# Attention output kept by token tiles and turned 128 channels at a time, with bias products once a bank and the last output projection by halves

## What is computed

```
x = x + 0.5 * ffn0(layernorm(x))          # ternary weights, silu gate, rms norm
x = x + attention0(layernorm(x))          # causal, ALiBi bias
x = x + 0.5 * ffn0(layernorm(x))
x = x + 0.5 * ffn1(layernorm(x))          # 2:4 sparsity of the hidden activations
x = x + attention1(layernorm(x))          # causal, rotary positions, biases on q, k, v and the output
x = x + 0.5 * ffn1(layernorm(x))

attention: q, k, v = projections of x                      (16 heads of 16 channels)
           p = softmax(q k^T / 4 + bias + causal mask)
           y = p v                                         (2048 x 256, heads side by side)
           out = y Wo (+ bo in attention1)
```

## Time and profile before

| | |
|---|---|
| median of three runs | 1694.61 us |
| the profiled execution | 1705.08 us, of which the span from first to last instruction is 1703.2 us |
| PE busy | 1543.7 us, 91% of the span |
| DVE, ACT, POOL busy | 73%, 56%, 12% |
| mean granted clock of PE | 0.945 of full speed |
| last places, tail and chain of the first attention | 632.94 to 701.82 us |
| the same of the second attention | 1467.44 to 1546.58 us |

### The profile page before, as it was taken

The page is one execution under the profiler, slowest core; times in us unless marked ns, Lnnn a source line. Parts: engine busy times, 40 slices in busy tenths (PEclk is TensorE's granted clock), DMA queues, the critical chain, the costliest instruction groups (busy, mean ns, idle before and its releaser), DMA issues. The chain is left out here.

```text
span 1703.2 us, 32639 instructions
## 1 busy us (share of the span) xinstructions
PE 1543.7 (91%) x13324; PEld 973.4 (57%) x13324; DVE 1242.4 (73%) x1735; ACT 945.8 (56%) x1891; POOL 208.7 (12%) x275
## 2 busy tenths in 40 slices
PE   2798788989999999899899598899999999998997
PEld 0687654444434446688688586544444444556887
DVE  7766457888898873566588886677888988433897
ACT  5454334757768875565344222456687688653442
POOL 0243000000000000156001032000000002200000
PEclk9999959999999999999999897779999999988999
DMA  5001969000000000200100076831101000000000
GB/s 212 25 0 15 186 148 127 26 13 25 14 13 14 2 2 1 75 1 1 37 1 1 16 140 179 106 51 46 47 24 32 14 2 2 2 1 1 2 25 26
DMA packets 38197, 70.61 MB, mean 41 GB/s; under 512 B 5490, under 2 KB 13298, under 8 KB 37236
## 3 DMA queue, kind: packets, MB, share of 16 engines
q1 hardware_dynamic: 38052, 68.58, 18.1%
HBM read 48.90 MB, written 22.15 MB: 42 GB/s over the span
## 5 line engine op out<-in xcount | busy, mean ns | idle before, releaser
L1333 DVE TENSOR_REDUCE l_att_maxima<-psum 128x2 f32<-128x1024 f32 (+3 forms) x640 | 665.2, 1063 | 141.0 <-PE psum L1130 132.5
L1501 ACT ACTIVATE l_att_probs<-psum 128x512 f32<-128x512 f32 (+3 forms) x1280 | 604.0, 532 | 287.0 <-PE psum L1160 266.0
L1177 PE MATMUL psum<-l_att_probs,l_att_v 128*17 128x256 f32 (+2 forms) x4608 | 353.1, 383 | 0.6
L1160 PE MATMUL psum<-l_att_qt,l_kt 51*128 51x512 f32 (+6 forms) x1280 | 318.2, 459 | 6.9 <-ACT l_att_probs L1501 6.7
L1130 PE MATMUL psum<-l_kt,l_att_qt 59*128 59x512 f32 (+7 forms) x1280 | 287.9, 427 | 5.1 <-DVE l_att_maxima L1333 3.3
L1160 PEld LDWEIGHTS psum<-l_att_qt,l_kt 59*128 59x128 f32 (+1 forms) x1280 | 137.1, 192 | 152.7 <-ACT l_att_probs L1501 141.2
L1177 PEld LDWEIGHTS psum<-l_att_probs,l_att_v 128*17 128x17 f32 x4608 | 82.1, 96 | 145.0 <-issue 93.6
L1130 PEld LDWEIGHTS psum<-l_kt,l_att_qt 59*128 59x128 f32 (+1 forms) x1280 | 140.9, 202 | 19.2 <-DVE l_att_maxima L1333 17.7
L358 PE MATMUL psum<-xh,w_ternary 128*128 128x512 f32 x256 | 104.0, 406 | 21.0 <-PEq L165 16.3
L1127 PE MATMUL psum<-tri 64*128 64x128 bf16 x1024 | 90.3, 240 | 24.4 <-DVE l_att_maxima L1333 17.4
L1456 POOL CAST l_att_crow<-l_att_cneg 128x16 bf16<-128x16 f32 x32 | 8.1, 254 | 807.6 <-DVE l_att_cneg L1343 807.6
(11 more groups left out here) (204 smaller groups left out, 2527.9 us busy)
## 6 DMA issues: line engine op xcount, KB each, us to landing
l_kt<-qk_scratch SPq DMA_DIRECT2D x48, 256.0 KB, 10.6
qk_scratch<-l_att_kv_parts SPq DMA_DIRECT2D x22, 512.0 KB, 8.6
l_att_qt<-qk_scratch SPq DMA_DIRECT2D x168, 64.0 KB
qk_scratch<-y SPq DMA_DIRECT2D x10, 512.0 KB, 13.4
set_raw<-in_w_gu SPq DMA_DIRECT2D x2, 1024.0 KB, 6.8
y<-in_w_gu SPq DMA_DIRECT2D x1, 2048.0 KB, 8.5
y<-in_rope SPq DMA_DIRECT2D x8, 256.0 KB, 6.4
l_att_w_raw<-in_w_gu SPq DMA_DIRECT2D x4, 512.0 KB, 3.8
```

Source lines behind the costliest of these rows:

```text
L1160: e.matmul(g.ps[:, score_bank(i), off:BLK], g.kt[rows_of(x), hp, kt * P:(kt + 1) * P], qt[rows_of(x), hp, off:BLK], start=u >= TPB, stop=True,
L1177: ins = e.matmul(g.ps[h * VW:h * VW + HD + 1, OB, lo:hi], g.v[:, kt, STEPS[st][1] * HG + h, :], pr[:, un % PB, h, lo:hi], start=u == 0 and ...
L1333: e.tensor_reduce(mp[:, st % 2, 2 * p:2 * p + 2, t, c], g.ps[:, bank:bank + 2, 0:w], AX.X, ALU.max).then_inc(s.mx, 1)
L1501: e.activation(pr[:, un % PB, h, off:BLK], g.ps[:, score_bank(i), off:BLK], ACT.Exp, scale=HD ** -0.5).then_inc(s.ex, 1)
```

## The change

It has four parts.

- `y` is laid out as 16 token tiles of 256 channels. `normalise` writes four pieces of 64 channels, 256 apart, for a step, and `turn` transposes a full 128x128 piece: four transposes give what eight products with the identity gave. A turn needs both head groups, so the turns of block 0 stand at the last two places ahead of the tail, and those of the other blocks at u = 2, 7, 12 (first 128 channels) and u = 5, 10 (the others), the latter ahead of the unit's `values`.
- In the second attention a bias product fills a whole bank of two token tiles (512 columns, the bias row read twice), and is the first product of the bank instead of the last of each tile. That holds for v and for the output.
- The last 128 channels of the last block (both groups, 14 and 15) go through transposes, `last_normalise`, turn, ACT copy, `last_split` and products in two halves of two token tiles, in banks of their own.
- The layer norm's turn moves from u = 10 to between the last two `values`. On DVE its statistics come after `split_turned(1, 1)`, its scaling (L128) after `split_turned(2, 1)`.

```
                 dst = g.ps[:, 6 + j // 2, (j % 2) * D:(j % 2 + 1) * D]
+                if rope and j % 2 == 0:
+                    e.matmul(g.ps[:, 6 + j // 2, :].rearrange("p (a d) -> p a d", a=2), g.one_row[:, :],
+                             g.brow[:, 0:D].unsqueeze(1).broadcast_to([HALF // 2 + 1, 2, D]),
+                             start=True, stop=False, skip_group_check=True)
                 todo = [(k, w, x) for k in range(KD) for w, x in terms]
                 for q, (k, w, x) in enumerate(todo):
                     ins = e.matmul(dst, xp[x][b % 2][:, k, j * P:(j + 1) * P], wq[w][:, k, 2 * D:3 * D],
-                                   start=q == 0, stop=not rope and q == len(todo) - 1)
-                if rope:
-                    ins = e.matmul(dst, g.one_row[:, :], g.brow[:, 0:D], start=False, stop=True)
+                                   start=q == 0 and not rope, stop=q == len(todo) - 1, skip_group_check=rope)
...
-        SHARED = ("T00", "T01", "O00", "T10", "O01", "Y14", "T11", "O10", "T20", "O11", "T21", "N0", "N1",
-                  "O20", "T30", "O21", "T31", "Y15")
+        SHARED = ("T00", "T01", "O00", "T10", "O01", "Y14", "T11", "O10", "T20", "O11", "T21", "O20", "T30", "O21",
+                  "N0", "N1", "U0", "U1")
+        HALVES = (slice(0, BLK // 2), slice(BLK // 2, BLK))
+        Y15 = (SB - 1, 2 * SB)
...
+        def heads_out(st, tiles):
+
+            qb, hg = STEPS[st]
+            rows = slice(qb * TPB + tiles[0], qb * TPB + tiles[-1] + 1)
+            return g.y[:, rows, hg * HG * HD:(hg + 1) * HG * HD].rearrange("p t (h d) -> p t h d", h=HG)
...
-            def turn(b, group, tiles):
-
-                item = f"T{b}{group // KD}"
-                r = group % (NG // KD) * HG * HD
-                if group % (NG // KD) == 0 and tiles[0] == 0:
-                    open_shared(item)
+            def turn_tiles(b, k, tiles, bank):
+
                 for j in tiles:
-                    ins = e.matmul(g.ps[r:r + HG * HD, shared_bank(item), j * P:(j + 1) * P], yv[:, b, group, j, :],
-                                   g.ident[:, :], start=True, stop=True)
-                if group % (NG // KD) and tiles[-1] == TPB - 1:
-                    ins.then_inc(s.yt, 1)
-                    released[item] = (s.ylo, KD * b + group // KD + 1)
+                    ins = e.transpose(g.ps[:, bank, j * P:(j + 1) * P],
+                                      g.y[:, b * TPB + j, k * P:(k + 1) * P], g.ident[:, :])
+                ins.then_inc(s.yt, 1)
+
+            def turn(b, k):
+
+                item = f"T{b}{k}"
+                turn_tiles(b, k, range(TPB), open_shared(item))
+                released[item] = (s.ylo, KD * b + k + 1)
+
+            def out_bias(bank):
+
+                e.matmul(g.ps[:, bank, :].rearrange("p (a d) -> p a d", a=2), g.one_row[:, :],
+                         g.brow[:, D:2 * D].unsqueeze(1).broadcast_to([HALF // 2 + 1, 2, D]),
+                         start=True, stop=False, skip_group_check=True)
 
             def out_product(b, j, bank, parts):
 
+                if rope and j % 2 == 0 and 0 in parts:
+                    out_bias(bank)
...
-                                       start=k == 0 and q == 0 and j % 2 == 0,
-                                       stop=not rope and k == KD - 1 and q == 2, skip_group_check=True)
-                if rope and KD - 1 in parts:
-                    ins = e.matmul(g.ps[:, bank, (j % 2) * D:(j % 2 + 1) * D], g.one_row[:, :], g.brow[:, D:2 * D],
-                                   start=False, stop=True, skip_group_check=True)
+                                       start=not rope and k == 0 and q == 0 and j % 2 == 0,
+                                       stop=k == KD - 1 and q == 2, skip_group_check=True)
...
-                if p >= 2 * TAIL - NG:
-                    turn(0, p - 2 * TAIL + NG, range(TPB))
+                if p >= 2 * TAIL - KD:
+                    turn(0, p - 2 * TAIL + KD)
...
+                if q == 0 and 0 < b < NB - 1:
+                    turn(b, 1)
                 if u:
                     values(un - DELAY, 0)
                 values(un - DELAY, 1)
                 if q == 2:
-                    turn(b + 1, 0, range(TPB))
-                    turn(b + 1, 1, range(TPB))
-                if q == 4 and b < NB - 2:
-                    turn(b + 1, 2, range(TPB))
-                    turn(b + 1, 3, range(TPB))
+                    turn(b + 1, 0)
                 if u == 3:
                     output_transposes(NS - 2, open_shared("Y14"))
                     released["Y14"] = (s.mx, read)
-                if u == 10:
-                    normal_turn(0)
-                    normal_turn(1)
-                if u == 14:
-                    turn(NB - 1, 2, range(TPB))
-            for un in range(UNITS - DELAY, UNITS):
-                values(un, 0)
-                values(un, 1)
+            values(UNITS - DELAY, 0)
+            values(UNITS - DELAY, 1)
+            normal_turn(0)
+            normal_turn(1)
+            values(UNITS - 1, 0)
+            values(UNITS - 1, 1)
             e.wait_ge(s.ylo, KD * NB - 1)
             for j in range(TPB):
                 out_product(NB - 1, j, j // 2, range(1))
-            output_transposes(NS - 1, open_shared("Y15"))
-            e.wait_ge(s.mx, read)
-            turn(NB - 1, 3, range(TPB))
-            e.wait_ge(s.ylo, KD * NB)
-            for j in range(TPB):
-                out_product(NB - 1, j, j // 2, range(1, KD))
+            e.wait_ge(s.ose, NS)
+            for half in range(2):
+                for t in range(2 * half, 2 * half + 2):
+                    ins = e.transpose(g.ps[:, Y15[half], t * P:(t + 1) * P], osb[:, t * P:(t + 1) * P], g.ident[:, :])
+                ins.then_inc(s.oth, 1)
+            for half in range(2):
+                e.wait_ge(s.yl, half + 1)
+                turn_tiles(NB - 1, 1, range(2 * half, 2 * half + 2), open_shared(f"U{half}"))
+            for half in range(2):
+                e.wait_ge(s.ylo, KD * NB + half)
+                for j in range(2 * half, 2 * half + 2):
+                    out_product(NB - 1, j, half, range(1, KD))
...
+            def last_normalise(half):
+
+                tiles = slice(2 * half, 2 * half + 2)
+                e.wait_ge(s.oth, half + 1)
+                po = g.ps[:, Y15[half], HALVES[half]].rearrange("p (t h w) -> p t h w", t=TPB // 2, h=HG)
+                e.reciprocal(rinv[:, tiles, :], po[:, :, :, HD]).then_inc(s.ri, 1)
+                e.wait_ge(s.ri, NS + half)
+                yv = heads_out(NS - 1, range(2 * half, 2 * half + 2))
+                e.tensor_tensor(yv, po[:, :, :, 0:HD], rinv[:, tiles, :].unsqueeze(3).broadcast_to([P, TPB // 2, HG, HD]),
+                                ALU.mult).then_inc(s.yl, 1)
+
+            def last_split(half):
+
+                hi, lo = out_parts(NB - 1, KD - 1)
+                e.wait_ge(s.yhi, KD * NB + half)
+                e.tensor_tensor(lo[:, HALVES[half]], g.ps[:, shared_bank(f"U{half}"), HALVES[half]], hi[:, HALVES[half]].bitcast(F32),
+                                ALU.subtract).then_inc(s.ylo, 1)
...
+            split_turned(1, 1)
             e.wait_ge(s.xres, 2)
             dve_stats(e, g, ln, 1, 0)
-            split_turned(1, 1)
-            dve_normalise(e, g, ln, 1, 0)
             residual(1, 0, shared_bank("O10"))
             split_turned(2, 0)
             residual(1, 1, shared_bank("O11"))
             split_turned(2, 1)
-            split_normal(0)
-            split_normal(1)
+            dve_normalise(e, g, ln, 1, 0)
             residual(2, 0, shared_bank("O20"))
             split_turned(3, 0)
             residual(2, 1, shared_bank("O21"))
-            normalise(NS - 1, shared_bank("Y15"))
-            split_turned(3, 1)
+            split_normal(0)
+            split_normal(1)
+            for half in range(2):
+                last_normalise(half)
+            for half in range(2):
+                last_split(half)
...
-            e.wait_ge(s.yt, KD * NB)
             e.wait_ge(s.po, 2 * (NB - 1))
-            e.activation(out_parts(NB - 1, KD - 1)[0], g.ps[:, shared_bank("T31"), :], ACT.Copy).then_inc(s.yhi, 1)
+            for half in range(2):
+                e.wait_ge(s.yt, KD * NB + half)
+                e.activation(out_parts(NB - 1, KD - 1)[0][:, HALVES[half]], g.ps[:, shared_bank(f"U{half}"), HALVES[half]],
+                             ACT.Copy).then_inc(s.yhi, 1)
...
-        g.y = sb("y", [P, NB * NG * TPB, HG * HD], F32)
+        g.y = sb("y", [P, NT, D], F32)
```

More of the change, by code:

```diff
@@ L963, in attention_phase @@
 def attention_phase(nc, g, name, rope, a, qx, splits, small, loads=()):
-    names = "ql qnext qrest amm mx cfin cm cp ct ctc cdma st ex pv ose ot ri yt yhi ylo po xres"
+    names = "ql qnext qrest amm mx cfin cm cp ct ctc cdma st ex pv ose ot ri yt yhi ylo po xres oth yl"
     names += " wraw whi wlo" if loads else ""
@@ L1213, in open_shared @@
                 return shared_bank(item)
```

(33 more changed lines are left out.)

## The result

The changed kernel took 1678.55 us (median of 4 runs, 1677.55 to 1681.10) against 1696.48 (4 runs, 1693.83 to 1699.49) of the kernel before on the same chip: a ratio of 0.988, 95% interval 0.985 to 0.991. Run again beside the experiments it took 1674.35 us (6 runs, 1664.71 to 1683.41), ratio 0.986 (0.982 to 0.990). The forecast was 1665, the range 1654 to 1681: faster and inside the range, but 9 to 14 us above the number.

A forecast was written before the change was run, and what follows sets the result against it. PE was taken to bound the tails, and latency the last chain. Two attentions at 11.1 us plus 4.3 for biases give 26.5, with 3 for clock: 1694.6 - 26.5 - 3 = 1665 us, range 1654 to 1681.

The forecast's parts named there:

- last chain: End of each attention, from step 15's transposes to the last addition: in halves 4.5 us instead of 6.32, gain 1.8.
- rival B: Four transposes of `y` cost 1.02 us like eight products, and halves give nothing: 1681 us, chance 0.11.
- turns ahead of the tail: Last four places before each attention's tail: two without a turn, two with four transposes, 5.2 instead of 8.0 us.
- tail with u = 6: Each attention's tail: cheaper turns gain 5.7 us, and a shorter wait in the scores of u = 6 gains 0.8.
- one attention: Sum for the first attention, 2.8 + 5.7 + 0.8 + 1.8 = 11.1 us; the second the same before its biases.
- biases of v: Second attention's v projection: one bias product for two tiles saves 0.39 us a bank, 2.3 us in three blocks.
- biases in the tail: Second attention's tail: gain between 0 and 0.39 us a bank, middle 0.2 taken for six banks, 1.2 us.
- biases in the chain: Second attention's last chain: four biases (2.0 us) leave, two of 0.61 come ahead of the transposes, gain 0.8 us.
- I take 3 us of these 11 as gain: Half-clock stretches in both tails and around the second chain's end cost 11 us; 3 us of it counted as gained.
- Rival A: The clock stays up in the tails and at the second chain's end, gaining all 11 us: 1657 us, chance 0.17.
- Rivals C and D: C: transposes cost clock at some turns, 1690, chance 0.05. D: lower clock through both tails, 1786 or 1727, chance 0.03.

The follow-up runs named there:

- biases alone: The kernel before with only the bias products of v and output made once a bank: 1695.12 us, ratio 0.996 to the kernel before.
- without the bias part: The changed kernel with bias products as before, one for each token tile, last: 1687.85 us, ratio 0.992 to the kernel before.
- turns as products: The changed kernel with `y` turned by ordinary products with the identity instead of transposes: 1691.85 us, ratio 0.992 to the kernel before.
- without halves: The changed kernel with the last block's end in one piece of four token tiles: 1673.85 us, ratio 0.983 to the kernel before.

## Why the prediction was right, and where it was wrong

The mechanism was right: a PE with nearly no idle time in the tails got faster by what its instructions cost less, and the last chain by halves. That the first time, 1678.55, fell inside the range owes something to luck and to the range's width: it is outside the forecast's own spread (1659 to 1673) and beside rival B's 1681, which the trace refutes.

The steps, all at 2.4 GHz, from the windows and rows above (before: first attention of "biases alone", which has the old code there, and the kernel with the output's biases once a bank for the second):

| step | predicted gain | measured |
|---|---|---|
| turns ahead of the tail | 2.8 | 2.7 (8.55 to 5.84) |
| tail with u = 6 | 6.5 | 6.15 (50.31 to 44.16), second 5.86 (51.31 to 45.45) |
| last chain | 1.8 | 1.47 (6.94 to 5.47) |
| one attention | 11.1 | 10.3 and 10.0 |
| biases of v | 2.3 | 2.4 (6 pairs by 0.40) |
| biases in the tail | 1.2 | 2.4 |
| biases in the chain | 0.8 | 0.8 |
| sum | 26.5 | 25.9 |

The last two rows are from the changed kernel with and without the bias part.

**Turns.** The price of a turn, 0.59 instead of 1.02, was right at every place shown, and turns as products gave the counter-proof. Rival B needed 1.02 for four transposes: refuted. ACT did become the limit at u = 6: the scores took 1.27, predicted about 1.1. ACT's eight exponentials are 4.22 us there, 0.2 longer than in the earlier trace rows, so its wait shrank by 0.7 and not by 0.8.

**Last chain.** 4.85 us instead of the predicted 4.5. The step that was off is the last one: DVE's and ACT's second halves came at their times (the turns of the second half ended at 1.9 after the transposes, ACT's copies at 2.3, the remainders at 2.8), but four tiles of products took 1.69 us from 684.76 on, not 1.5, and had started 0.2 late, at 2.4.

**Biases.** The middle of 0 to 0.39 a bank was too low: 2.4 us for six banks are 0.4. Twelve biases of 0.31 us (3.7) left the tail, so six for two tiles each added 1.3 in all (by difference, 0.2 each; the one shown takes 0.38 from start to start), where the prediction had 0.61 each for the v tiles.

**Clock.** This is the step that failed: "I take 3 us of these 11 as gain". Those stretches went altogether: in none of the 12 tails turned by transposes was there one, while of the four executions of the old code with biases per tile three had one in the second tail and four in its chain. But of the ten other tails of the old code one had such a stretch, although the long scores of u = 6 are there too (in the kernel with only the output's biases once a bank 1.97 us at 1499.50, in the tail of clock 1.00 shown above). So the long scores alone don't bring the stretch, and which part of the change took it away is not shown. And I let the rest of the execution keep its clock, while its lower stretches move by more than the step was worth. Rival A, that all 11 come, was no better: it has the tails right and the sum wrong. The first profile after had 23 us of lower clock less in tails and chain and 30 more elsewhere. How far runs scatter with the clock can be read from the runs with a clock on record: within one kernel a run whose mean granted clock is 0.001 lower is 1.06 us longer (a common slope over 86 runs). Taken to one clock, 0.945, the means are 1702.0 (before, 39 runs), 1694.8 (biases alone, 9), 1683.5 (turns as products, 10), 1681.0 (without the bias part, 11), 1675.3 (without halves, 4) and 1672.7 us (changed, 11), each to about 1 us. That is 29.4 us between the two kernels. At their own clocks (means 0.9458 and 0.9430) the means are 26.4 apart, and the medians of the first four runs 17.9. At one clock the differences are larger than the steps above (29.4 against 25.9 for the whole, 8.3 against 5.6 for the biases, 10.8 against 7.4 for the turns as products), and what the rest is stays open. So does whether the clock itself moved with the edits: the means without the bias part (0.9401) and with turns as products (0.9392) are below that of the kernel before by more than three times their uncertainty, that of the changed kernel by 1.6 times. The number of the forecast was within what the clock moves from run to run.

Rivals C and D are refuted. The windows of tails and chains after have a clock of 1.00 with all turns by transposes, and turns as products were not better clocked (tails 1.00 too, the whole 0.9392 against 0.9430). The Trainium skill says in "TensorE: Matmul & The Clock Gate", section "Part 4: PE-mode transpose", that transposes do not count as PE-busy as matmuls do; here, with 0.59 us of them at a time between products, no effect of that was to be seen, and the measurement decides for this use.

## What to carry to other kernels

Where PE is the bound, price an edit by start-to-start times of the same instruction from the trace: five of six steps came out within 0.4 us that way in the first attention and the biases. Before explaining a difference between two traces by the edit, compare stages that the edit doesn't touch, with the granted clock beside the length, and profile each kernel three times. An edit worth 2 us of 1700, as the halves, shows only in the trace of its own stage, not in the time.

## What was not expected of the hardware

- A kernel on one core repeated a stage of 400 us with nothing edited at 398.0 to 415.7 us. The stretches at 1.2 GHz, some 3 to 44 us each, lie in part at other places in each execution.
- A turn of [128 x 512] in float32 is 1.09 us by ordinary products, recorded as eight, and 0.59 us by transposes, recorded as four.
- A bias product of 33 rows for one tile costs 0.50 us in a v tile, 0.51 between output products (0.86 against 0.35), and 0.31 ahead of the values, whose shape differs anyway. One of 512 columns for two v tiles in place of two of 256 saves 0.40.
